# Pairwise attention of a perceiver layer: the rows that subtract the maxima move from 64-row products of each unit to sets of four 32-row products, one set for two units

## The reference, cut to what matters

```python
q = jnp.einsum('bld,ed->ble', lat, Wq)
kv_in = jnp.concatenate((x, lat), axis=-2)
kv = jnp.einsum('bld,ed->ble', kv_in, Wkv)
k, v = jnp.split(kv, 2, axis=-1)
...
attn_scale = 1.0 / np.sqrt(np.sqrt(DIM_HEAD)).astype(np.float32)
logits = jnp.einsum('bhqd,bhkd->bhqk', q * attn_scale, k * attn_scale)
w = jax.nn.softmax(logits.astype(jnp.float32), axis=-1).astype(logits.dtype)
out = jnp.einsum('bhqk,bhkd->bhqd', w, v)
```

## Time and profile before

| what | value |
|---|---|
| median of three runs | 3549.62 us (3545.74 to 3551.71) |
| the profiled execution | 3550.18 us |
| its span, first to last instruction | 3548.5 us |
| PE busy | 3184.4 us, 90% |
| DVE, ACT, POOL busy | 2474.4, 1690.0, 1872.4 us |
| exponentials of the attention (L2021) | 944 |
| 64-row products with the maxima (L1931, `pair_q_shift`) | 1888 |
| reductions of the fills (L2070) | 1800 |

### The profile page before, as it was taken

The page is one execution under the profiler, slowest core; times in us unless marked ns, Lnnn a source line. Parts: engine busy times, 40 slices in busy tenths (PEclk is TensorE's granted clock), DMA queues, the critical chain, the costliest instruction groups (busy, mean ns, idle before and its releaser), DMA issues. The chain is left out here.

```text
span 3548.5 us, 51026 instructions
## 1 busy us (share of the span) xinstructions
PE 3184.4 (90%) x18472; PEld 1860.8 (52%) x18472; DVE 2474.4 (70%) x4297; ACT 1690.0 (48%) x2048; POOL 1872.4 (53%) x1158
## 2 busy tenths in 40 slices
PE   5979797586448999999999999999999999999977
PEld 3757575332324555555555555555555555555435
DVE  6979797653258776877777777687777777768431
ACT  5758585243213444454444444445444444444432
POOL 3857575111222655655655565565565566556750
PEclk8989898566679999999999999999999999999988
DMA  1000000000410000000000000000000000000000
GB/s 62 1 1 1 1 1 1 12 1 1 139 21 3 1 1 1 4 1 1 4 1 1 1 4 1 1 4 1 1 4 1 1 1 2 1 1 1 1 26 7
DMA packets 20416, 28.21 MB, mean 8 GB/s; under 512 B 5064, under 2 KB 12368, under 8 KB 20048
## 3 DMA queue, kind: packets, MB, share of 16 engines
q1 hardware_dynamic: 18832, 21.83, 1.9%
q0 software_dynamic: 1344, 3.15, 0.3%
HBM read 21.30 MB, written 3.67 MB: 7 GB/s over the span
## 5 line engine op out<-in xcount | busy, mean ns | idle before, releaser
L2021 ACT ACTIVATE pair_probs<-banks 128x1024 f32<-128x1024 f32 (+1 forms) x944 | 965.7, 1026 | 1035.8 <-PE banks L1931 983.9
L2070 DVE TENSOR_REDUCE pair_peaks<-banks 128x1 f32<-128x512 f32 (+1 forms) x1800 | 1086.4, 666 | 271.3 <-PE banks L1913 257.9
L2163 POOL TENSOR_TENSOR pair_total_pool<-pair_total_pool,pair_probs 128x1536 f32<-128x1536 f32 x208 | 724.5, 3483 | 754.2 <-DVE pair_total L2084 749.0
L1954 PE MATMUL banks<-pair_probs,pair_values 128*64 128x512 f32 (+1 forms) x3776 | 872.9, 600 | 0.0
L1913 PE MATMUL banks<-pair_k_high,pair_q_high 64*128 64x512 f32 (+1 forms) x1920 | 567.3, 442 | 27.3 <-DVE pair_peaks L2063 14.8
L2152 POOL TENSOR_TENSOR pair_total_pool<-pair_total_pool,pair_probs 128x1024 f32<-128x1024 f32 x224 | 536.0, 2393 | 39.1 <-POOL pair_total_pool L2163 21.5
L2084 DVE TENSOR_TENSOR pair_total<-pair_total,pair_probs 128x512 f32<-128x512 f32 (+2 forms) x464 | 458.2, 988 | 94.3 <-ACT pair_probs L2021 69.1
L1954 PEld LDWEIGHTS banks<-pair_probs,pair_values 128*64 128x64 f32 (+1 forms) x3776 | 248.3, 136 | 472.8 <-issue 384.9
L1931 PE MATMUL banks<-pair_q_shift,pair_one_rows 64*128 64x512 f32 (+1 forms) x1888 | 476.1, 396 | 3.1 <-ACT pair_probs L2021 3.1
L1913 PEld LDWEIGHTS banks<-pair_k_high,pair_q_high 64*128 64x128 f32 x1920 | 262.8, 184 | 356.1 <-issue 212.3
L1931 PE MATMUL banks<-pair_q_high,pair_k_high 64*128 64x512 f32 (+1 forms) x1888 | 427.5, 391 | 0.0
(11 more groups left out here) (325 smaller groups left out, 3776.3 us busy)
## 6 DMA issues: line engine op xcount, KB each, us to landing
expert_w<-in_fc SPq DMA_DIRECT2D x32, 256.0 KB, 3.6
context_rows<-in_ctx SPq DMA_DIRECT2D x10, 320.0 KB, 6.7
dense_w<-in_We SPq DMA_DIRECT2D x2, 1024.0 KB
experts_in<-expert_zeros SPq DMA_DIRECT2D x1, 1024.0 KB, 3.8
expert_b<-in_fc_b SPq DMA_DIRECT2D x2, 512.0 KB, 5.0
expert_rows<-experts_in SPq DMA_DIRECT2D x16, 64.0 KB, 1.9
experts_out<-expert_result POOLq DMA_DIRECT2D x4, 256.0 KB, 3.7
row_parameters<-in_rows SPq DMA_DIRECT2D x1, 896.0 KB, 8.7
```

Of the source, the lines that this page charges most:

```text
L1954: last = pe.matmul(out[heads[head], :], values[0:n, ring_of(h // 2, i // 4), i % 4, heads[head]], probs_of(h, i)[0:n, head, :], start=i == ...
L2021: act.activation(probs_of(h, i)[0:n], slot(e)[0:n], ACT.Exp, scale=1.0 / 8.0).then_inc(S["expd"].sem, 1)
L2070: v.reduce_max(peaks[:, head, t, b:b + 1], fill_bank(f, head)[:, 0:width(b)], axis=AX).then_inc(S["peaked"].sem, 1)
L2163: pool.tensor_tensor(pooled[:], pooled[:], three, ALU.add).then_inc(S["pooled"].sem, 1)
```

## The change

The fourth product of a unit is taken out of pairs of neighbouring units (0 and 1, 2 and 3 of a step) and replaced by one set of four products of 32 rows for both units. `pair_lane_rows` has ones in rows 0, 32, 64 and 96, and VectorE writes the negated maxima to rows 0, 32, 64 and 96 of `pair_q_shift` instead of 0 and 64. The set's products go to four different banks: both heads of both units. For units 0 and 1 the set comes ahead of unit 0 and opens the four sums. For units 2 and 3 it comes between them: it closes the sums of unit 2 and opens those of unit 3. For the set TensorE waits until the slot of the second unit (`partner`) is free too. Left as they were are the unit of 4 keys and units 0 and 1 of a step that follows on an `output` or `denominators` entry.

```diff
-def turns_of(place):
+def turns_of(products, place):
 
-    lanes = [[(head, m) for m in range(4)] for head in range(2)]
+    lanes = [[(head, m) for m in products] for head in range(2)]
...
+    for n, e in enumerate(entries[:-1]):
+        if e[0] == "scores" and e[2] % 4 in FIRST_OF_TWO and entries[n + 1][0:2] == e[0:2] and e[2] < TILES \
+                and entries[n + 1][2] // 4 == e[2] // 4 and entries[n - 1][0] not in ("output", "denominators"):
+            partner[e] = entries[n + 1]
+    second = set(partner.values())
...
+                for row in range(0, P, LANE):
+                    v.memset(lane_rows[row:row + 1].bitcast(F32), 1.0).then_inc(S["cleared"].sem, 1)
...
+                def share_shift(units, ends):
+                    for u, unit in enumerate(units):
+                        n = parts_of(unit[2])
+                        for head in range(2):
+                            lane = slice(head * HD1 + u * LANE, head * HD1 + (u + 1) * LANE)
+                            last = pe.matmul(slot(unit)[0:n, head, :], lane_rows[lane, 0:n], q_shift[lane, :],
+                                             start=u == 1 or not ends, stop=u == 0 and ends)
+                        if u == 0 and ends:
+                            last.then_inc(S["made"].sem, 1)
+
                 def scores(e, h, i, f):
-                    wait_free(e)
+                    if e not in second:
+                        wait_free(e)
...
+                    ends = e in partner and i % 4 == 2
+                    if e in partner and not ends:
+                        wait_free(partner[e])
+                        share_shift((e, partner[e]), ends)
...
+                    products = range(1, 4) if e in partner or e in second else range(4)
...
+                    if ends:
+                        wait_free(partner[e])
+                        share_shift((e, partner[e]), ends)
...
-                        v.reduce_max(peak_columns, peaks[:], axis=AX).then_inc(S["largest"].sem, 1)
+                        v.reduce_max(largest[:], peaks[:], axis=AX).then_inc(S["largest"].sem, 1)
                         wait(v, "largest", h + 1)
-                        v.tensor_scalar(peak_columns, peak_columns, -1.0, None, ALU.mult).then_inc(S["negated"].sem, 1)
+                        for columns in peak_columns:
+                            v.tensor_scalar(columns, largest[:], -1.0, None, ALU.mult).then_inc(S["negated"].sem, 1)
```

More of the change, by code:

```diff
@@ L1660 @@
 PLACES = ((0, 0), (0, 1), (0, 0), (0, 2))
-def turns_of(place):
-    lanes = [[(head, m) for m in range(4)] for head in range(2)]
+LANE = 32
+FIRST_OF_TWO = (0, 2)
+def turns_of(products, place):
+    lanes = [[(head, m) for m in products] for head in range(2)]
     for head in range(2):
-        lanes[head].insert(place[head], ("fill", head))
+        if place is not None:
+            lanes[head].insert(place[head], ("fill", head))
     return [turn for both in zip(*lanes) for turn in both]
@@ L1759, in perceiver_attention @@
     scored = {e[1:3]: number[e] for e in entries if e[0] == "scores"}
+    partner = {}
+    for n, e in enumerate(entries[:-1]):
[3 more added lines that the diff above has]
+    second = set(partner.values())
     fills = []
@@ L1776, in perceiver_attention @@
         one_rows = k.sb("pair_one_rows", [P, P], F32R, ctx=ctx)
+        lane_rows = k.sb("pair_lane_rows", [P, P], F32R, ctx=ctx)
+        largest = k.sb("pair_largest", [P, 2, TQ], ctx=ctx)
         probs = k.sb("pair_probs", [P, 2, 4, 2, HALF], ctx=ctx)
@@ L1791, in perceiver_attention @@
         heads = (slice(0, HD1), slice(HD1, P))
-        peak_columns = peak[:].rearrange("p (n c) -> p n c", c=TQ)[:, 0:HD1 // TQ + 1:HD1 // TQ, :]
+        peak_columns = [peak[:].rearrange("p (n c) -> p n c", c=TQ)[:, lane // TQ:(lane + HD1) // TQ + 1:HD1 // TQ, :]
+                        for lane in (0, LANE)]
         def wait(engine, name, n):
@@ L1829, in _ @@
                 v.memset(peak[:], 0.0).then_inc(S["cleared"].sem, 1)
-                wait(v, "cleared", 2)
+                v.memset(lane_rows[:].bitcast(F32), 0.0).then_inc(S["cleared"].sem, 1)
+                wait(v, "cleared", 3)
                 for row in (0, HD1):
                     v.memset(one_rows[row:row + 1].bitcast(F32), 1.0).then_inc(S["cleared"].sem, 1)
-                wait(v, "cleared", 4)
+                for row in range(0, P, LANE):
+                    v.memset(lane_rows[row:row + 1].bitcast(F32), 1.0).then_inc(S["cleared"].sem, 1)
+                wait(v, "cleared", 9)
         with nc.Block() as block:
@@ L1930, in product @@
                         right = (q_shift, q_high[h % 2], q_high[h % 2], q_low[h % 2])[m][heads[head], :]
[L1931 to L1935, removed]
+                        return pe.matmul(slot(e)[0:n, head, :], left, right, start=m == (1 if ends else 0),
+                                         stop=m == 3 and not ends)
+                    products = range(1, 4) if e in partner or e in second else range(4)
+                    turns = turns_of(products, None if f is None else PLACES[i % 4])
                     final = [turn for turn in turns if turn[0] != "fill"][-1]
@@ L1939, in scores @@
                             fill(f, turn[1])
-                        elif turn == final:
+                        elif turn == final and not ends:
                             product(*turn).then_inc(S["made"].sem, 1)
@@ L1959, in shift @@
                     wait_free(e)
-                    wait(pe, "negated", number["peak", h])
+                    wait(pe, "negated", 2 * number["peak", h])
                     for t in range(TQ):
```

## The result

The changed kernel takes **3653.85 us** in the median of four runs (3650.61 to 3655.16), the kernel before 3549.05 (3545.74 to 3551.71, four runs). The ratio is 1.0294, 95% interval 1.0277 to 1.0312. I had forecast 3648.

A forecast was written before the change was run, and what follows sets the result against it. TensorE sets the pace, busy 2314 of 2351 us in the units' stretch; 91.0 + 4.5 + 4.7 - 3.5 + 1.2 = 97.9 us on 3550.2 gives 3648 us, own range 3630 to 3670 (60%).

The forecast's parts named there:

- The boundary's price: Wherever TensorE's array changes shape, even in rows alone, the next product comes 0.43 us later instead of 0.23: 0.20 us each.
- Four products at once: In each set the four 32-row products run together and take the time of one pair, 0.23 us.
- The chain at unit 2: Unit 2 waits for unit 0's exponential, 0.20 us later, then its second fill product waits 0.15 for VectorE's third reduction.
- the first rival: Drains cost but VectorE's wait at unit 2 hides: 0.35 us a full step, 27 us less, 3621 us; chance 16%.
- A full step: A step with both sets and with fills takes 0.50 us more; 182 of them make 91.0 us.
- The steps with the second set alone: Full steps with only the set between units 2 and 3, 2 in 15 halves: 30 x 0.15 = 4.5 us.
- the sixteenth half, steps with both sets: In the half without fills, 12 steps lose 0.39 us each, 4.7 us, as the set waits for the second exponential.
- last steps of the halves: The set fits into the fourth fill product's wait for a reduction, so a pair is saved: 15 x -0.23 = -3.5 us.
- around: Outside the steps, five more memsets cost some 1.0 us and a second negation in the first half 0.2: 1.2 us.
- The faster rival: Passing between 64 and 32 rows does not drain the array, so set boundaries cost zero: 3525 us; chance 9%.
- The slower one: A set's four products run two after two and take two pairs' time, 100 us more: 3748 us; chance 8%.
- the load of unit 2 released by VectorE: Sign in the changed profile: unit 2's weight load (PEld L1928) released by DVE `pair_peaks` instead of ACT.

The follow-up runs named there:

- the kernel with 32-row pairs: Against the kernel before, no sets; in unit 2 of every step the two products with the maxima use 32 rows instead of 64: 3631.69 us, ratio 1.0225.
- The repeated set: Against the changed kernel, each set issued twice in a row without a change of shape between: 3749.87 us, ratio 1.0559.
- the run with the second sets: Against the kernel before, only the sets between units 2 and 3; units 0 and 1 keep their 64-row turns: 3596.5 us, ratio 1.0126.
- the set behind unit 3: Against the kernel before, only sets for units 2 and 3, each placed behind unit 3 and closing all four sums: 3711.18 us, ratio 1.0451.

## Why the prediction was right

**The boundary's price, 0.20 us.** It rested on one row, the load at 2000.67 from 128 to 4 rows. The changed kernel has 0.43 to 0.44 us from a set to what follows against 0.23 in the shape, 0.32 us from the last start in the old shape to the set's load as forecast, and the kernel with 32-row pairs pays 80.8 us for two of them in unit 2; I had expected 88.

**Four products at once.** No row before showed this; I had taken it from the pairs. The repeated set settled it at 0.24 us.

**The chain at unit 2.** Predicted: exponential later by 0.20, then VectorE by 0.15. Shown: unit 2's first load 2.75 us behind the step's first instead of 2.54, the second head's load 0.16 to 0.17 later and 0.05 us behind the third reduction's end, and 28 us back when that fill stands one turn later, against the 27 of the first rival's sum. That rival, that VectorE hides, is out.

**A full step.** Forecast 0.50 us. The one shown has 9.20 - 8.65 = 0.55, the mean is 0.54. This is the term that was too small, by 0.04 us a step. It is spread evenly: from the step's first load to the late load of unit 2 I had 2.89 us and the rows after give 2063.12 - 2060.20 = 2.92; from there to the load of the next shape I had 2.67 and they give 2065.82 - 2063.12 = 2.70. Five boundaries and twelve turns were added up from rows rounded to 0.01 us.

**Seven full steps that cost nothing.** I counted 182 of them, and only 175 pay. In the seven odd halves 1 to 13 (counted from 0) the first step ends in the products of `denominators`, and there TensorE had waited for GpSimd's sums. In the first such half, before and after:

```profile
1244.54 1.12 PE L1891 MATMUL banks<-keys_normed_turned,pair_wk 128*128 128x512 f32 x2
1246.37 1.08 PE L1969 MATMUL banks<-pair_total_pool,ones 128*64 128x512 f32 x4 [0.71 <-POOL pair_total_pool L2135]
...
1253.46 1.12 PE L1906 MATMUL banks<-keys_normed_turned,pair_wk 128*128 128x512 f32 x2
1254.73 1.08 PE L2002 MATMUL banks<-pair_total_pool,ones 128*64 128x512 f32 x4
```

From `produce` to these products it was 1.83 us and is 1.27: the half microsecond that the step lost before them went into the wait. The wait stood in the earlier trace rows (10.7 us, 9 times) and I didn't use it. After the change that row is:

```profile
PE banks L2002 <- POOL pair_total_pool L2169: 5.8, 2, 5.1
```

**The steps with the second set alone.** I had 0.15 us and they cost 0.20, part of it the wait for unit 1's exponential that the run with the second sets shows. I had held this wait to be over in the full step, where it is, and didn't ask in these.

**The terms side by side**, in us over the span of the profiled execution, read from load to load:

| term | forecast | measured |
|---|---|---|
| full steps with both sets, with fills | 91.0 (182 x 0.50) | 94.2 (175, each 0.54) |
| steps with the second set alone | 4.5 | 6.0 |
| the sixteenth half, steps with both sets | 4.7 | 4.8 |
| last steps of the halves | -3.5 | -3.6, and +0.2 in the sixteenth |
| around | 1.2 | 1.0 |
| sum | 97.9 | 102.6 (the spans: 3651.1 - 3548.5) |

So the mechanism held and the forecast is 5 us short. The number has a little luck in it: the full step's error of 7 us was cut by half by the seven steps whose loss was hidden.

**The faster rival**, free passage between 64 and 32 rows, is refuted by the 32-row pairs. **The slower one**, two after two, by the repeated set.

**What I named as a sign and didn't find**: the load of unit 2 released by VectorE. The merged row still names ScalarE, since the first head's load was released by it. The width of the row, 0.35 us instead of 0.18, was the sign. The load behind the set stands 0.43 us behind the set's own load; the 0.32 us that I gave count from the start of its products, as in the replay.

Where a forecast of mine did fail is the set behind unit 3: I checked whom the moved work waits for and not who waits for the slot that it now holds longer.

## What to carry to other kernels

Packing four small products into the row groups of the array works, but a change of shape costs nearly as much as the turn it saves, 0.20 us against 0.23. A visit to the other shape adds two changes, 0.40 us, and each set in it saves 0.23. By an estimate from these numbers it takes two sets in one visit to come out ahead on TensorE's own time; no run here has tried it. So gather the products of one shape; on the trace, look at the distance between a product and the first load of another shape before costing anything by its own duration.

A product that moves ahead of others delays all that hangs on them: here the first sets, which cost nothing by a count of TensorE's own time, made more than half of the loss (58.8 of 104.4 us) through an exponential and a bank. And a loss ahead of a wait for another engine can vanish in it, as in the seven steps above.

## What the runs showed of the hardware

The price of a boundary was the same for every kind seen here: 0.43 us from one product to the next in both directions between 64 and 32 rows, and the same 0.81 us of idle loads ahead of the set behind the float32 products as ahead of the 64-row fill before. Of the 0.20 us, 0.09 to 0.10 is that the load comes 0.32 to 0.33 us behind the last start in the old shape and not 0.23, and 0.11 the load that nothing covers. I had not expected four products in four row groups to keep so exactly to the pace of two: 0.24 us for a set inside its shape, against 0.23 for a pair.
